# Gated cross-attention and a mixture of experts: the attention part rewritten for two heads in the two row halves of PE

## The chip, the cores and the metric

The kernel runs on one core of a Trainium2 chip. What counts is the device time of one launch in microseconds. PE is the matrix engine (TensorE), DVE the vector engine, ACT the scalar engine, POOL is GpSimd, and SP is the queue that issues the DMAs here.

## What is computed

```python
# x (4, 1024, 256); ctx (4, 154, 256); 16 heads of 16
q = layernorm(x) @ Wq.T / 4;  k = ctx @ Wk.T;  v = ctx @ Wv.T       # per head
d = clip(i - j, -4, 4) + 4                                           # i query, j key
scores = q @ k.T + (q @ p_params)[i, d];  scores = where(i >= j, scores, -1e30)
x = x + tanh(g_xattn) * (softmax(scores) @ v) @ Wo.T
h = layernorm(x);  s = sigmoid(h @ gate_w.T)      # 8 experts, 4 chosen through groups, plus a shared one
y = sum over chosen e of w_e * (silu(h @ Wg[e]) * (h @ Wu[e])) @ Wd[e] + shared(h)
x = x + tanh(g_ffn) * y
```

With 154 keys and 1024 queries, only the first 158 queries see a mask or a bias that depends on the distance; from then on every distance is clipped, and the bias of distance 4 is folded into the keys (`rel[:, 2 * DIST:]` is added to them). Two tiles of 128 queries per batch item, tiles 0 and 1, need corrections.

## The kernel before

A batch item has 1024 queries in two halves of 512. Attention runs in 8 units, one per batch item `b` and half `h` (`u = 2b + h`); an even unit (h = 0) holds the two corrected tiles. A unit has 20 steps on PE, five for each group of four heads: four score products with the keys as stationary operand and 512 queries moving (256 in an even unit), and one short chunk for the keys beyond 128, of four heads together (`score`, L892). ACT takes the exponential of each (L503), and PE multiplies by the values in four strips of 32 columns (`values`, L938 and L942). In the same steps PE works ahead: from step 3 on, two products a step give the scores of the next unit the other way round (queries stationary), only for the row maxima (`max_scores`, `stack_scores`, L877), through a ring of three PSUM banks that DVE empties (`maximum`, L604). Transposes of x (L811), queries (L853), keys (L822) and values (L837, L839) of the unit after next, the transposes of the maxima (L889, step 19) and the output projection of the unit before (L953, step 19) are put between the steps by hand. Each engine follows a list of steps of its own; PE, ACT and DVE run in order, so that one late wait holds up all that stands behind it.

Matmul operands are split in a high and a low part of type fp32r, and three products replace one in fp32. Heads go in stacks of two: `qs` holds for a stack 96 rows (two heads of 16 dimensions, in three copies: high, low, high), `km` the keys of both heads in 308 columns, block-diagonal, so that one product over 96 rows gives both heads; rows 96 to 127 carry the negated maxima, picked by one-hot rows in `ks`. The copies are made by DMAs from `qh`, `ql` (`q_stack`, 12 DMAs of 128 KB a unit) and from `km` (`k_stack`).

In an even unit the two corrected tiles go another way: ACT copies their scores from PSUM to `sx` (L486), POOL builds the band of bias corrections `d0`, `d1` from the products with `p_params` that stand in eight further columns (`near`, L388 to L411), DVE adds them and takes the maxima (`tile0`, `tile1`, L619 to L640), POOL and DVE subtract these, and PE transposes the result back into the score banks (L917, L922). The units of items 1 and 2 run in a loop (`Fori`), the others are written out.

The softmax divisors travel through DRAM and come back inverted and broadcast (`divisors`, 8 DMAs to `at`); DVE multiplies (`divide`, L671), PE projects, and DVE adds to x (L678). Behind attention, PE first projects unit 6, then turns to the experts' transposes (L1418), router (L1426) and 72 expert items of 24 matmuls each.

## Time and profile before

| | us |
|---|---|
| median of 3 runs | 726.85 (726.72 to 727.78) |
| profiled execution | 730.77 |
| its span | 728.7 |
| PE busy | 619.2 (85%) |
| DVE busy | 458.8 (63%) |
| ACT busy | 276.1 (38%) |
| POOL busy | 178.3 (24%) |

The busy times and all rows are of the one profiled execution. A busy PE is modelled: a matmul's record holds its latency too, so durations of neighbours overlap, and the rate is read from start to start. PEld are the loads of the stationary operand. In the name of a matmul, 96\*128 are the rows and columns of the array that it uses, and 96x308 what moves through. An fp32 matmul leaves two records.

### The profile page before, as it was taken

Reading aid. Unit: us, or ns where it says so; the run is one execution under the profiler, and the core shown is the slowest. Engines: PE = TensorE matmul, PEld = TensorE weight load, DVE = VectorE, ACT = ScalarE, POOL = GpSimd, SP = SyncE. Lnnn points to the kernel's source line nnn. Section 1 sums busy time; section 2 is a strip of 40 time slices with the busy share of each in tenths; the row PEclk is TensorE's granted clock in tenths of the full one; section 3 lists DMA queues with packets and bytes.
Section 4 is the critical chain, followed back from the end, with each engine's and each line's share of the span. In section 5 each row is a group of like instructions: output and inputs, shape, how many; then the busy total and the mean of one; then the engine's idle time right before and its main releaser. Section 6 shows DMA issues by size and latency. Waiting matters only on the chain.

```text
span 728.7 us, 10636 instructions
## 1 busy us (share of the span) xinstructions
PE 619.2 (85%) x3384; PEld 485.6 (67%) x3384; DVE 458.8 (63%) x884; ACT 276.1 (38%) x501; POOL 178.3 (24%) x177
## 2 busy tenths in 40 slices
PE   2665968788978987878667999999999999999997
PEld 2544745566645755554345888888888887888886
DVE  3677657868587758761277575756657475765653
ACT  2432456334733455344351422333242332324222
POOL 2151005300341007100111232232324223232222
PEclk9976989999989999999869999999999999999999
DMA  6850233524252333473212022031212202121220
GB/s 223 210 133 23 45 73 88 124 46 98 60 130 62 74 86 88 106 231 74 47 31 86 32 66 81 2 102 43 87 58 73 72 8 94 43 87 59 74 73 29
DMA packets 39856, 58.65 MB, mean 80 GB/s; under 512 B 7984, under 2 KB 21040, under 8 KB 39792
## 3 DMA queue, kind: packets, MB, share of 16 engines
q1 hardware_dynamic: 39824, 58.25, 28.9%
q8 instruction: 17, 0.28, 0.2%
q14 instruction: 15, 0.12, 0.0%
HBM read 31.76 MB, written 4.85 MB: 50 GB/s over the span
## 4 chain that ended last, share of the span: by engine, by line
issue 49%; PE 21%; DVE 11%; POOL 8%; DMA 5%; ACT 3%; SPq 2%; DVEq 0%; POOLq 0%; ACTq 0%
POOL hl L1172 4%; PE oT L938 3%; PE smax L877 3%; PE sT L918 3%; PE oT L942 3%; DMA qs<-mt 3%; DVE mx L604 2%; PE work L822 2%; SPq L296 2%; POOL d L399 2%; DVE mx L632 1%; PE sT L917 1%; DMA at<-rden_d 1%; PE work L853 1%; PE work L811 1%
## 5 line engine op out<-in xcount | busy, mean ns | idle before, releaser
L1172 POOL TENSOR_TENSOR hl<-sg,hh 128x512 fp32r<-128x512 f32 x72 | 93.2, 1296 | 249.6 <-ACT hh L1215 249.6
L503 ACT ACTIVATE ex<-sT 128x512 f32<-128x512 f32 (+1 forms) x160 | 91.9, 593 | 156.2 <-PE sT L918 130.7
L1209 ACT ACTIVATE sg<-pg 128x512 f32<-128x512 f32 x72 | 43.1, 598 | 199.2 <-PE pu L1455 198.4
L877 PE MATMUL smax<-km,qs 96*128 96x308 f32 (+1 forms) x244 | 86.9, 393 | 26.3 <-DVE mx L604 19.0
L604 DVE TENSOR_REDUCE mx<-smax 128x2 f32<-128x308 f32 x185 | 81.0, 472 | 35.8 <-PE smax L877 34.8
L877 PEld LDWEIGHTS smax<-km,qs 96*128 96x128 f32 x244 | 48.7, 209 | 60.5 <-DVE mx L604 35.4
L1470 PE MATMUL py<-wxl,hh 128*128 128x256 f32 x288 | 81.9, 284 | 4.2 <-DVE x L1353 3.1
L1470 PE MATMUL py<-wxh,hl 128*128 128x256 f32 x288 | 80.8, 281 | 0.0
L1470 PE MATMUL py<-wxh,hh 128*128 128x256 f32 x288 | 80.6, 280 | 0.0
L1341 DVE TENSOR_TENSOR sg<-cwb,sg 128x512 f32<-128x512 f32 x64 | 66.6, 1040 | 10.8 <-DMA cwb<-cwt_d 7.9
L1336 DVE TENSOR_TENSOR sg<-pu,sg 128x512 f32<-128x512 f32 x72 | 49.2, 684 | 28.4 <-ACT sg L1209 26.9
L918 PE MATMUL sT<-qs,ks 128*128 128x256 f32 (+1 forms) x128 | 53.4, 434 | 13.0 <-DMA qs<-mt 11.7
L1455 PE MATMUL pg<-x2l,wxh 128*128 128x512 f32 x144 | 60.3, 419 | 4.1 <-issue 4.1
L1470 PEld LDWEIGHTS py<-wxl,hh 128*128 128x128 f32 x288 | 54.3, 188 | 10.2 <-DVE x L1353 5.4
L1455 PE MATMUL pu<-x2l,wxh 128*128 128x512 f32 x144 | 57.9, 402 | 0.0
L1455 PE MATMUL pu<-x2h,wxl 128*128 128x512 f32 x144 | 57.8, 401 | 0.0
L1455 PE MATMUL pg<-x2h,wxh 128*128 128x512 f32 x144 | 57.6, 400 | 0.0
L1455 PE MATMUL pg<-x2h,wxl 128*128 128x512 f32 x144 | 57.5, 399 | 0.0
L1455 PE MATMUL pu<-x2h,wxh 128*128 128x512 f32 x144 | 57.3, 398 | 0.0
L1470 PEld LDWEIGHTS py<-wxh,hl 128*128 128x128 f32 x288 | 54.2, 188 | 2.7
L1470 PEld LDWEIGHTS py<-wxh,hh 128*128 128x128 f32 x288 | 54.6, 190 | 0.0
L1215 ACT CAST hh<-sg 128x512 fp32r<-128x512 f32 x72 | 44.0, 611 | 9.6 <-DVE sg L1341 9.3
(154 smaller groups left out, 1125.8 us busy)
## 6 DMA issues: line engine op xcount, KB each, us to landing
cwb<-cwt_d SPq DMA_DIRECT2D x64, 256.0 KB, 3.3
qs<-qh SPq DMA_DIRECT2D x64, 128.0 KB, 2.5
qs<-ql SPq DMA_DIRECT2D x32, 128.0 KB, 2.5
at<-rden_d SPq DMA_DIRECT2D x64, 64.0 KB, 2.2
out<-x SPq DMA_DIRECT2D x8, 512.0 KB, 4.3
ks<-km SPq DMA_DIRECT2D x16, 231.0 KB, 3.4
wx<-in_wx SPq DMA_DIRECT2D x9, 384.0 KB, 6.2
x<-in_x SPq DMA_DIRECT2D x3, 1024.0 KB, 8.6
```

Of the source, the lines that this page charges most:

```text
L503: nc.scalar.activation(ex[:, g % 2, i % 5, q0:HALF], ST[i % 2][:, q0:HALF], ACT.Exp).then_inc(exp_s, 1)
L604: nc.vector.reduce_max(mx[:, m_tile(h, p), 2 * stk:2 * stk + 2], banks[q % len(banks)][:, 0:PAIR].rearrange("p (j k) -> p j k", j=2), AX_X)\
L877: last_one = nc.tensor.matmul(bank[:, 0:width], qs[0:96, s, tile * P:(tile + 1) * P], km[:, s, 0:width], start=True, stop=True)
L918: last_one = nc.tensor.matmul(out[:, q0:HALF], ks[:, s, j * KL:j * KL + P], qs[:, s, q], start=True, stop=True)
L938: nc.tensor.matmul(OT[32 * j:32 * j + 32, :], va[:, 4 * g + j, :], ex[:, g % 2, j, :], start=True, stop=True)
L1172: nc.gpsimd.tensor_tensor(hl[:, i % R, :], sg[:, i % R, :], hh[:, i % R, :], ALU.subtract).then_inc(hl_done, 1)
L1209: nc.scalar.activation(sg[:, i % R, :], PG[i % RG][:], ACT.Silu).then_inc(sg_s, 1)
L1215: nc.scalar.copy(hh[:, i % R, :], sg[:, i % R, :]).then_inc(hh_s, 1)
L1336: done = nc.vector.tensor_tensor(sg[:, i % R, :], PU[i % RG][:], sg[:, i % R, :], ALU.mult)
L1341: nc.vector.tensor_tensor(sg[:, i % R, :], cwb[:, e % RC, :], sg[:, i % R, :], ALU.mult)\
L1455: last = nc.tensor.matmul(out_[:], wa[:, e, w], xa[:, u, c, :], start=first, stop=(c == C - 1 and wa is wxh and xa is xh))
L1470: last = nc.tensor.matmul(y, ha[:, i % R, q], wa[:, e, 2 * C * I:XW], start=(e == 0 and s == 0 and j % 2 == 0), stop=(e == NE1 - 1 and s = ...
```

## The change

The attention part is rewritten; the experts keep their items. In the diff:

- The heads of a stack lie apart: one in rows 0 to 63, the other in rows 64 to 127 of `qs` and `ks` (48 rows of high, low, high, two rows with the maxima's high and low part, zeros up to 64). A stack's scores are two products over 50 rows each, in the two halves (`score_pair`), of 124 keys and always 512 queries; the short chunk takes the other 30 keys. The products for the maxima (`fill`) are four in a step for steps 0 to 15, of 154 columns over 48 rows, into two banks that one reduction of DVE empties; the next `fill` waits for that reduction. Score banks are three instead of two, exponentials are kept in nine places.
- Corrections: POOL makes the bands `d0`, `d1` in a high and a low part, causal mask included, from products of their own (`relative`, 12 of 32 columns); PE adds them to the scores with the identity as the other operand (`added`, and the second part of `fill`). `sx`, the copies by ACT and the additions and subtractions on it are gone.
- Queries and keys are written to DRAM and read back in the new order (`q_store`, `q_stack`, `k_stack`), into three buffers for queries and two for keys. Keys are projected in 4 products instead of 16.
- In the head, the loads of x for items 1 to 3 come behind the stacks and six DMAs that write zeros to the unused rows (14 rows of 16 KB each); DVE waits for all three before its first reduction.
- The loop is gone: all units are written out. The maxima's transposes are in step 17, the output projections in 18 and 19. The divisors come back in one DMA, and POOL divides.
- Behind attention, the experts' first transposes are ahead of the projection of unit 6, and what DVE does for the router comes behind its first statistics.

```diff
-        sp.wait_ge(kv_in, 3 * 16)
-        for i in range(1, B):
-            sp.dma_start(x1[:, i * NT:(i + 1) * NT, :], t["x"][i]).then_inc(x_in[i], 16)
...
+        def q_store(u, part):
+            sp.dma_start(q_d[u, part], (qh, ql)[part][:].rearrange("p c n -> p (c n)").bitcast(F32)).then_inc(qd_out, 16)
+        def q_stack(u):
+            sp.wait_ge(qd_out, 32 * (u + 1))
+            if u > 2:
+                sp.wait_ge(st_ps, NEV * (u - 2))
+            for r in range(3):
+                rows = q_d[u, r % 2].rearrange("(s d) (a n) -> a d s n", d=HD, a=2)
+                for a in range(2):
+                    at_row = ROW * a + HD * r
+                    sp.dma_start(qs(u)[at_row:at_row + HD, :, :].bitcast(F32), rows[a]).then_inc(qs_in, 16)
...
+        def m_stack(u):
+            sp.wait_ge(mT_s, u + 1)
+            for a in range(2):
+                for part in range(2):
+                    at_row = ROW * a + KQ + part
+                    sp.dma_start(qs(u)[at_row:at_row + 1, :, :].bitcast(F32),
+                                 mt[H * part + a:H * (part + 1):2, :].bitcast(F32)).then_inc(ms_in, 16)
...
+        sp.wait_ge(q_hi, 2)
+        q_store(0, 0)
+        sp.wait_ge(work_free, freed("q", 0, 1))
+        q_store(0, 1)
+        q_stack(0)
+        sp.wait_ge(pool_set, 6)
+        k_stack(0)
+        zeros = k2[0:ROW - KS, :, :].rearrange("p s k -> p (s k)").bitcast(F32)
+        for i in range(RQ):
+            for a in range(2):
+                sp.dma_start(q_buf[i][ROW * a + KS:ROW * (a + 1), :, :].rearrange("p s n -> p (s n)").bitcast(F32)
+                             .rearrange("p (r k) -> p r k", r=4),
+                             zeros.unsqueeze(1).broadcast_to([ROW - KS, 4, NSTK * P])).then_inc(fill_in, 16)
+        for i in range(1, B):
+            sp.dma_start(x1[:, i * NT:(i + 1) * NT, :], t["x"][i]).then_inc(x_in[i], 16)
+        sp.wait_ge(v_ps, 1)
+        sp.dma_start(ctxb[:], t["ctx"][1]).then_inc(c_in, 16)
+        sp.wait_ge(work_free, freed("q", 1, 1))
+        q_store(1, 0)
+        q_store(1, 1)
+        q_stack(1)
+        m_stack(0)
...
+            nc.vector.reduce_max(mx[:, tile, 4 * sp:4 * sp + 4].rearrange("p (s a) -> p a s", a=2),
+                                 SM[:, :, 0:PAIR].rearrange("p a (s k) -> p a s k", s=2)[:, :, :, 0:keys],
+                                 AX_X).then_inc(mx_s, 1)
...
         for i in range(1, B):
             dve.wait_ge(x_in[i], 16)
+        tile_stats(2)
+        norm_stats(2)
+        for f in range(NFILL):
+            maximum(0, f)
+        minus_max(0)
+        max_out(0)
         dve.wait_ge(g_set, 1)
...
+        def fill(u, f):
+            h, b = u % 2, u // 2
+            tile, sp = fill_of(h, f)
+            if f == 0:
+                pe.wait_ge(qs_in, 6 * 16 * (u + 1))
+                pe.wait_ge(ks_in, 6 * 16 * (b + 1))
+            if u > 0 or f > 0:
+                pe.wait_ge(mx_s, NFILL * u + f)
+            edge = tile if h == 0 else 2
+            keys = P if edge == 0 else KL
+            for s in (2 * sp, 2 * sp + 1):
+                for a in range(2):
+                    rows = slice(ROW * a, ROW * a + KQ)
+                    last_one = nc.tensor.matmul(SM[:, a, s % 2 * KL:s % 2 * KL + keys], qs(u)[rows, s, tile * P:(tile + 1) * P],
+                                                ks(b)[rows, s, 0:keys], start=True, stop=True)
+            if edge < 2:
+                if f % 4 == 0:
+                    pe.wait_ge(d_s, NDS * b + (NDS if edge == 0 else 3))
+                for a in range(2):
+                    both = SM[:, a, 0:PAIR].rearrange("p (s k) -> p s k", s=2)
+                    heads = slice(4 * sp + a, 4 * sp + 4, 2)
+                    for part in range(2):
+                        if edge == 0:
+                            last_one = nc.tensor.matmul(both[:, :, 0:P], idr[:], d0[part][:, heads, :], start=False, stop=True,
+                                                        skip_group_check=True)
+                        else:
+                            last_one = nc.tensor.matmul(both[:, :, KM:KL], idr[:], d1[part][:, heads, 0:K1], start=False,
+                                                        stop=True, skip_group_check=True)
             last_one.then_inc(sm_ps, 1)
...
+        def added(out, keys, q, corrections):
+            for part in corrections:
+                last = nc.tensor.matmul(out[0:keys, q], part, idr[:, q.start % P:(q.stop - 1) % P + 1], start=False,
+                                        stop=True, skip_group_check=True)
+            return last
...
+        def score_pair(u, s):
+            n = NI * u + 5 * (s // 2) + 2 * (s % 2)
+            h, b = u % 2, u // 2
+            if n > 1:
+                pe.wait_ge(exp_s, n - 1)
+            if s == 0:
+                pe.wait_ge(ms_in, 64 * (u + 1))
+                pe.wait_ge(fill_in, 2 * RQ * 16)
+            for a in range(2):
+                rows = slice(ROW * a, ROW * a + KS)
+                last_one = nc.tensor.matmul(ST[0:KM, (n + a) % 3, :], ks(b)[rows, s, 0:KM], qs(u)[rows, s, :],
+                                            start=True, stop=True)
...
+                for a in range(2):
+                    last_one = added(ST[:, (n + a) % 3, :], KM, slice(0, P), [part[:, 2 * s + a, 0:KM] for part in d0])
+            last_one.then_inc(st_ps, 1)
...
+            out = ST[:, n % 3, :]
+            q0 = KM if h == 0 else 0
+            for k in range(2):
+                last_one = nc.tensor.matmul(out[:, q0:HALF], k2[:, 2 * g + k, :], qs(u)[:, 2 * g + k, q0:HALF],
+                                            start=(k == 0), stop=(k == 1))
+            if h == 0:
+                heads = slice(4 * g, 4 * g + 4)
+                added(out, P, slice(KM, P), [part[:, heads, :] for part in d0s])
+                last_one = added(out, P, slice(P, 2 * P), [part[:, heads, :] for part in d1])
+            last_one.then_inc(st_ps, 1)
...
+        def unit(u):
+            b = u // 2
+            ahead = u < NU - 2
             for i in range(NI):
-                seeks = 0 <= i - M0 < NM and (h == 0 or ahead)
-                score(b, h, i, start)
-                if seeks:
-                    max_scores(b + h, 1 - h, i - M0, 0)
-                if i in (1, 3) and carry:
-                    values(b - 1 + h, 1 - h, NG - 1, i // 2)
+                if i % 5 in (0, 2):
+                    score_pair(u, 2 * (i // 5) + i % 5 // 2)
+                elif i % 5 == 4:
+                    score_short(u, i // 5)
+                if i in (1, 3) and u > 0:
+                    values(u - 1, NG - 1, i // 2)
                 if i > 5 and i % 5 in (1, 3):
-                    values(b, h, i // 5 - 1, i % 5 // 2, start)
-                if seeks:
-                    max_scores(b + h, 1 - h, i - M0, 1)
-                if i in (5, 6) and ahead:
-                    transposes(u + 2, b, X_USE[h], (i - 5,))
-                if i in (7, 8) and ahead and h == 0:
-                    values_in(b + 1, b, V_USE, ((0, 1), (2, 3, 4))[i - 7])
-                if i in (9, 10, 11, 12) and ahead:
-                    queries(b, X_USE[h], Q_USE[h], (i - 9,))
-                if ahead and h == 0:
-                    keys(b + 1, b, K_USE, [s for s in range(NSTK) if K_STEP[s] == i])
-                if i == 19:
-                    if h == 0 or ahead:
-                        max_T(b + h, 1 - h, b, M_USE[h])
-                    if carry and (h == 0 or ahead):
-                        for pr in range(2):
-                            project(b - 1 + h, 1 - h, pr, b, Y_USE[h] + pr)
+                    values(u, i // 5 - 1, i % 5 // 2)
+                if u < NU - 1 and i < NFILL:
+                    fill(u + 1, i)
+                if ahead and i == K_PE and u % 2 == 0:
+                    keys(b + 1)
+                if ahead and i in X_PE:
+                    transposes(u + 2, X_PE.index(i))
+                if ahead and i in Q_PE:
+                    queries(u + 2, Q_PE.index(i) // 2, (Q_PE.index(i) % 2,))
+                if ahead and i == RV_PE:
+                    if u % 2:
+                        values_in(b + 1)
+                    else:
+                        relative(b + 1)
+                if i == NFILL + 1 and u < NU - 1:
+                    max_T(u + 1)
+                if i in (18, 19) and 0 < u < NU - 1:
+                    project(u - 1, i - 18)
```

## Rows read from the trace of the kernel before

**Rows 1.** Busy time by stage: length, then each engine's busy time, granted clock, DMA.

```profile
core 0: us, PE busy (x) PEld busy (x) DVE busy (x) ACT busy (x) POOL busy (x), PEclk, DMA share, GB/s
62.60:332.90 270.30, 220.94 (x1225) 154.48 (x1225) 192.05 (x363) 126.63 (x245) 52.62 (x60) 0.93 0.37 92
...
351.00:382.30 31.30, 19.54 (x59) 13.89 (x60) 18.16 (x52) 12.21 (x19) 3.91 (x5) 0.67 0.13 28
382.30:728.70 346.40, 332.94 (x1904) 287.12 (x1902) 211.91 (x394) 107.41 (x179) 102.27 (x84) 0.99 0.19 61
```

**Rows 2.** Waits of PE, 62.6 to 332.9: in total, times, longest.

```profile
PE smax L877 <- DVE mx L604: 19.0, 8, 3.9
...
PE sT L918 <- DMA qs<-mt: 11.7, 4, 5.4
```

**Rows 3.** Instructions in order of time, PE, 182 to 190: start, duration, instruction.

```profile
182.17 1.06 PE L938 MATMUL oT<-ex,va 128*32 128x512 f32 x8
183.17 0.73 PE L918 MATMUL sT<-qs,ks 128*128 128x512 f32 x2
183.74 0.31 PE L877 MATMUL smax<-km,qs 96*128 96x316 f32 x1
183.88 0.29 PE L880 MATMUL smax<-cmask,idr 128*128 128x256 f32 x1
184.01 0.81 PE L942 MATMUL oT<-ex,vb 128*128 128x384 f32 x2
...
189.84 0.60 PE L811 MATMUL work<-idr,xn 128*128 128x128 f32 x4
```

**Rows 4.** In order of time, 193.9 to 198, around a change to column strips.

```profile
193.93 3.65 POOL L399 TENSOR_TENSOR d<-relr,cst 128x2048 f32<-128x2048 f32 x1
...
195.72 0.39 PE L918 MATMUL sT<-qs,ks 128*128 128x512 f32 x1
...
195.95 0.30 PE L877 MATMUL smax<-km,qs 96*128 96x316 f32 x1
...
196.18 0.16 PEld L938 LDWEIGHTS oT<-ex,va 128*32 128x32 f32 x8 [0.27 <-issue]
196.18 1.06 PE L938 MATMUL oT<-ex,va 128*32 128x512 f32 x8
...
197.18 0.42 PE L877 MATMUL smax<-km,qs 96*128 96x316 f32 x1
...
197.44 0.39 PE L853 MATMUL work<-xth,wql 128*128 128x512 f32 x1
```

**Rows 5.** In order of time, the head up to the first score.

```profile
20.12 3.44 PE L822 MATMUL work<-ctxb,wk 128*96 128x154 f32 x24
...
21.65 1.38 SPq L267 DMA_DIRECT2D qs<-qh  x2
...
39.91 0.85 DVE L604 TENSOR_REDUCE mx<-smax 128x2 f32<-128x308 f32 x2
...
62.93 0.56 PE L918 MATMUL sT<-qs,ks 128*128 128x256 f32 x1
```

**Rows 6.** DMA issues of the page: KB each, median time to landing.

```profile
qs<-qh SPq DMA_DIRECT2D x64, 128.0 KB, 2.5
```

**Rows 7.** DMAs that load x, 0 to 30: duration of issue, first and last start.

```profile
L260 SPq DMA_DIRECT2D x<-in_x x3: 378/583/1469, 13.6 to 14.6; - x3
...
DMA to landing us min/median/max: 4.6/7.8/12.1
```

**Rows 8.** In order of time, between attention and experts.

```profile
355.45 1.40 DVE L1253 BATCH_NORM_STATS2 stats<-x 128x6 f32<-128x256 f32 x4
...
358.61 6.72 PE L953 MATMUL work<-wo,at 128*128 128x256 f32 x16 [4.37 <-DVE at L671]
...
372.38 0.80 PE L1426 MATMUL pm<-x2l,gst 128*128 128x512 f32 x1 [1.40 <-DVE x2l L1269]
```

More of the change, by code:

```diff
@@ L21 @@
 KL = 154
-K1 = KL - P
 KPAD = 160
@@ L431, in gpsimd @@
-        batches(pool, unit)
+        rotated(0)
+        near(0)
+        values(0)
+        rstd_of(2)
+        for u in range(NU):
+            unit(u)
+        return lambda: divide(NU - 2), lambda: divide(NU - 1)
     def scalar(act):
@@ L523, in scalar @@
[L523 to L537 removed]
+            nc.scalar.copy(kept(u)[:, g, :], OT[:]).then_inc(raw_s, 1)
```

1148 lines of the change are left out of this document (517 added, 631 removed).

## Prediction

> **What bounds the kernel now.** I read the busy time by stage first [rows 1]. It tells three things. The expert stage from 382.3 us on takes 346.4 us with PE busy 332.9 of them at a granted clock of 0.99; the change touches none of its loop, so it moves as a block. The middle of attention, from the first score to the last unit (62.6 to 332.9, 270.3 us for seven of eight units, about 39 us each), has PE busy 220.9, DVE 192.1, ACT 126.6: PE is the fullest engine and no other is near it, but PE also stands still for 49 us. What is left is a head of 62.6 us before the first score and a passage of 31.3 us between attention and the experts, in which PE is busy 19.5 us at a clock of 0.67. I then asked what PE waits for in the middle [rows 2]: 19.0 us for DVE to reduce the maxima, 11.7 us at the starts of units for the DMA that brings the negated maxima. Last I looked at single matmuls for prices [rows 3, 4], and at the head and the passage in order of time [rows 5 to 8]. So attention is bound by the order of work on PE, with two waits in it; the head is bound by a chain over ACT, DVE and POOL; and whatever the change does, 346 us stay.
>
> **Prices, at full clock.** Start to start: 512 columns in fp32r 0.23 us (195.72 to 195.95); 308 or 316 columns 0.14 (183.74 to 183.88); 256 columns 0.13 (183.88 to 184.01) [rows 3, 4]. An fp32 transpose of 128 columns 0.11 (four in 0.60 less the tail of the last) [rows 3]. Four heads' values in the four column strips of PE 1.0 (182.17 to 183.17). An fp32 key projection of 154 columns 0.29, as two records of 0.14 each (24 in 3.44) [rows 5]. No fp32r matmul under 256 columns stands in the trace, and none in the upper or lower half of the rows. Bounds for one of 154 or 128 columns: below, in proportion to the 308-column row, 0.07; above, the fp32 key row, 0.29. I take 0.12: a 256-column matmul with a new stationary block of 128 columns takes 0.13, so the block can be exchanged in that time, and the 308-column row is of the same operands. For a pair of heads in the two halves I take one such time, not two, since in the column strips the eight records of four heads run together (eight weight loads in 0.16 us [rows 4]).
>
> **What a change of tiling costs.** From full rows to strips: 195.95 to 196.18 is 0.23 for a matmul of 0.14, so 0.09 more. Back: 197.18 to 197.44 is 0.26 for one of 0.14, so 0.12 more for the next weight load, which could not be brought forward [rows 4]. Some 0.1 per change, then, between bounds of 0 (if halves need no such drain; the trace has column strips only) and 0.2. The Trainium skill says the same and against this change: its page TensorEngine Tiling (Array Packing), section Tiling Modes, has it that a change of tiling mode, not only of tile, drains the engine. By that rule every passage from halves to full rows is paid; the strips' rows agree, and halves no row shows.
>
> **Units, part by part.** Common to both versions, per unit: values, query projections, transposes of x, output projection. What differs, in us of PE:
> Even unit before: 16 heads of two transposes and a 256-column score, 16 x 0.34 = 5.4; four short chunks 1.4; 32 stacks of maxima 4.6; keys, 32 records of 0.14, 4.6: 16.0. After: 8 pairs of 512 columns 1.9; 32 corrections of 128 columns 3.8; four short chunks with four corrections 3.4; 32 pairs for the maxima 3.8; keys 4 x 0.29 = 1.2; the new relative products, 12 x 0.12 = 1.4: 15.5.
> Odd unit before: scores 3.7, short chunks 1.9, maxima with eight masks 5.6: 11.2. After: pairs 1.9, short chunks 1.9, maxima 3.8, 32 corrections to their edge tiles 3.8: 11.4.
> So the halving of scores is spent on corrections: 0.2 us saved per unit. The changes of tiling: fills alternate with values, chunks, corrections and projections in each of 16 steps, about 45 passages per unit against 8; 37 x 0.11 = 4.1 more. The waits: one reduction of 616 elements per step, in place of two of 308 (0.85 for two [rows 5]), on one pair of banks where there was a ring of three; a fill waits for the reduction of the step before, most of which lies under 1 us and more of other PE work: from 2.7 us per unit (19.0 over seven) to about 1. The maxima leave two steps earlier, before both output projections: of 1.7 us per unit (11.7 over seven) 0.5 stay. Late next is the query projection at step 4: its operand is subtracted on DVE only behind the reduction of the same step, 0.85 + 0.7 us: 1.0 more. Together -0.2 + 4.1 - 1.7 - 1.2 + 1.0 = +2.0 per unit, by 6.5 units (the first has no output projection, the seventh no projections ahead) +13. DVE loses the additions and subtractions on whole score tiles and the division, POOL and ACT their parts of it; none of that ends last, so beyond the waits it is worth nothing. Divisions go to POOL behind the band work (two of the 3.65 us row [rows 4], a mask of the same shape as much, and the small ones): about 15 of 39 us, done before the projection at step 18. Loops written out add instructions to fetch; no row prices it, 0 to 3 us, I take 0.
>
> **The head.** Before, three loads of x (1 MB each) are issued at 13.6 to 14.6 and the slowest lands after 12.1 us [rows 7]; the first score is at 62.93 [rows 5]. After, SP issues them only behind the stores of queries and keys to DRAM, the wait for these, six plus six stack loads and six zero fills of 224 KB. From the queries' end at 21.65 [rows 5]: store and return 2.5, the landing time of a stack load of 128 KB [rows 6], six loads at 0.6 each (two in 1.38 [rows 5]) to 28, keys' store and return to 31.5, six loads to 35, fills to 39, x to 41. Then 1.3 + 3 MB at the pace of the 12.1 us row: landed near 53. DVE waits for all three before its first reduction, then does 1.8 us of statistics: 54 or 55. PE stands with one fill made and its clock falls, as in the passage (0.67 [rows 1]). Sixteen fills then take turns with sixteen reductions, nothing overlapping: 0.85 reduction, 0.5 matmuls at half clock, 0.25 handing over, 1.6 x 16 = 26, and 1.0 for the corrections of eight: 33. At 87 come transposes, copy and DMA, about 4 (an estimate; PE's wait for such a DMA was 2.9 in the mean, 11.7 over four [rows 2]): first score at 91, 28 later. Low bound: x landed at 47, turns of 1.2: +12; high +36. I take +26.
>
> **The end.** DVE's statistics for the experts start at 355.45, having waited for ACT's last copy; PE does 16 records of output projection (6.72 us at half clock, 358.61 to 365.3) ahead of the transposes; the router starts at 372.38 [rows 8]. After, statistics wait for nothing (351), transposes come first, the division is on POOL after rstd near 357, projection until 364, router right behind: 8 us earlier, and the last unit, with three banks in place of two, perhaps 1. The weights' DMA stands ahead of the divisors in SP's queue and lands some 9 us into the last unit, early enough. I take -8 (-2 to -12).
>
> **Sum.** 730.8 (span 728.7 and 2.1 around it) + 26 + 13 - 8 = 761.8. The profiled execution was 3.9 above the median shown, 726.85, so 758.
>
> **Rivals.** (a) PE runs free. If a change between halves and full rows costs nothing (-4.1), a pair of fills passes in 0.08 (-1.3), no fill waits (-1.0) and the clock stays up (0.93 in the middle: -1.5), a unit is 5.9 us shorter, -38 in all; with a head of +22 and -8: 730.8 - 24 - 3.9, about 703, faster. For it: 49 us of PE's idleness and DVE's load of 192 us are what the change removes. Against: the head. (b) Short fp32r matmuls at the fp32 price: 32 pairs at 0.26 and 128-column corrections at 0.21, +6.4 per unit, +42: 800. For it: no row under 256 columns; against: nothing in the 308-column row hints at it. (c) The halves don't run side by side, so the change doesn't do what it says: 32 x 0.12 and 8 x 0.23 more, +5.7 per unit, +37: 795. The Trainium skill is against (c): TensorE: Matmul & The Clock Gate, Part 3, measures four row tiles of 32 at 3.07 times one. (d) Head and units cancel, 727: the head at +12 with units at -0.6 each.
>
> **How the numbers follow.** Forecast 758, chance 0.40, own range 738 to 778. (a) 0.29, (b) 0.17, (c) 0.09, (d) 0.05. 0.2% of this kernel is 1.5 us, about what its measurement tells from no change. Faster: (a) and the low edge of (d), 0.31; same 0.04; slower 0.65. Range 700 to 802: below lies part of (a), above part of (b).
>
> **What would show it.** Head: first reduction right after x's third landing near 53, fills and reductions in turn, first score near 91; if it is under 75 the forecast falls. Units: start to start of a fill behind a full-row matmul 0.1 over the same without a passage; two heads' records starting within 0.02 (else (c)); 154 columns at 0.12 and not 0.26 (else (b)); unit length 41 and not 34 (else (a)). End: transposes ahead of the projection, router near 13 us after the last score instead of 21.

## The result, and the profile after

| | before | after |
|---|---|---|
| median of the runs, us | 727.3 (4 runs, 726.7 to 729.0) | 895.8 (4 runs, 893.8 to 899.1) |
| profiled span, us | 728.7 | 892.4 |
| head, to the first exponential | 63.5 | 115.3 |
| units 0 to 6 | 269.9 (38.6 each) | 386.8 (55.3 each) |
| last unit | 18.1 | 16.3 |
| from there to the experts' first gate | 30.8 | 27.8 |
| experts | 346.4 | 346.2 |

The ratio is 1.2322 (95% interval 1.2284 to 1.2361): 168 us slower, where 31 were forecast. Rows are of one execution of each kernel; those of e7 below are of its slowest (798.9 us, its median is 788.3), so that a comparison with them overstates what another kernel gained on it by up to 10 us. The span grew by 163.7: head +51.8, units +116.9, the end -4.8. The stages of after, with the columns of [rows 1]:

```profile
114.00:502.10 388.10, 315.95 (x1544) 195.41 (x1546) 163.46 (x254) 105.41 (x207) 79.28 (x67) 0.71 0.35 64
518.40:546.20 27.80, 16.66 (x59) 12.39 (x60) 16.80 (x43) 11.78 (x18) 8.64 (x8) 0.75 0.23 52
546.20:892.40 346.20, 333.81 (x1904) 288.05 (x1902) 212.36 (x398) 107.31 (x179) 102.06 (x84) 0.99 0.19 61
```

DVE did become lighter (163 us against 192 in [rows 1]), and the time did not follow. The granted clock in the units fell from 0.93 to 0.71, that is, PE spent more than half of the time at 1.2 GHz and the rest at 2.4. What PE waited for in the units of after, as [rows 2]:

```profile
PE sT L883 <- issue: 35.7, 6, 9.1
PE work L775 <- DVE xn L590: 19.3, 3, 10.3
PE work L809 <- DVE xtl L595: 9.7, 6, 1.8
PE smax L841 <- DVE mx L642: 5.9, 16, 0.5
PE sT L883 <- DMA qs<-mt: 5.1, 1, 5.1
```

The wait for reductions fell from 19.0 to 5.9 us, as forecast. The first row is the first score of a unit, which waits for the maxima's DMA; "issue" only means that the profile found no releaser. In order of time, PE and SP's queue show it:

```profile
268.78 2.69 SPq L271 DMA_DIRECT2D qs<-q_d  x6
...
271.66 1.89 PE L937 MATMUL work<-wo,at 128*128 128x256 f32 x8
...
271.91 2.72 SPq L294 DMA_DIRECT2D qs<-mt  x4
...
274.13 1.94 PE L937 MATMUL work<-wo,at 128*128 128x256 f32 x8
...
285.17 0.79 PE L883 MATMUL sT<-qs,ks 50*124 50x512 f32 x2 [9.10 <-issue]
```

Six copies of a query stack (1.5 MB) are issued just ahead of the four small DMAs; the last of the six lands 12.9 us after its own issue, 15.1 after that of the first. The second row of waits is this, DVE, POOL and PE in order of time:

```profile
170.21 0.80 DVE L642 TENSOR_REDUCE mx<-smax 128x4 f32<-128x616 f32 x1 [5.07 <-PE smax L841]
170.50 3.63 POOL L425 TENSOR_TENSOR d0h<-relr_h,cst 128x2048 fp32r<-128x2048 f32 x1
170.92 11.89 DVE L590 TENSOR_SCALAR xn<-x,mv,rstd 128x256 f32<-128x256 f32 x4
...
174.21 4.49 POOL L432 TENSOR_TENSOR d0h<-d0h,cst 128x2048 fp32r<-128x2048 f32 x1
178.66 3.69 POOL L425 TENSOR_TENSOR d0l<-relr_l,cst 128x2048 fp32r<-128x2048 f32 x1
...
182.97 1.08 PE L775 MATMUL work<-idr,xn 128*128 128x128 f32 x4 [10.32 <-DVE xn L590]
```

Four operations of 0.41 us took 11.89 together: the first three each end 0.15 us after one of POOL's, the fourth takes 0.40 again. The head in order of time, where [rows 5] had the reductions at 39.91:

```profile
44.08 11.31 SPq L352 DMA_DIRECT2D qs<-k  x6
...
55.44 7.34 SPq L356 DMA_DIRECT2D x<-in_x  x3
...
72.05 1.41 DVE L575 BATCH_NORM_STATS2 stats<-x 128x6 f32<-128x256 f32 x4 [39.96 <-DMA x<-in_x]
...
76.21 0.71 PE L841 MATMUL smax<-ks,qs 48*128 48x154 f32 x4 [0.89 <-DVE mx L642]
76.96 0.80 DVE L642 TENSOR_REDUCE mx<-smax 128x4 f32<-128x616 f32 x1 [0.81 <-PE smax L841]
77.81 0.71 PE L841 MATMUL smax<-ks,qs 48*128 48x154 f32 x4 [0.90 <-DVE mx L642]
```

The turns are 1.6 us, as forecast. What came late is x. Last, PE at the full clock around its changes of tiling, and the end (compare [rows 8]):

```profile
261.85 0.45 PE L841 MATMUL smax<-ks,qs 48*128 48x154 f32 x4
...
262.14 0.43 PE L883 MATMUL sT<-qs,ks 50*124 50x512 f32 x2
...
262.50 0.32 PE L868 MATMUL sT<-idr,d0h 128*124 128x128 f32 x1
...
262.65 0.27 PE L868 MATMUL sT<-idr,d0l 128*124 128x128 f32 x1
...
262.87 0.27 PE L868 MATMUL sT<-idr,d0l 128*124 128x128 f32 x1
...
263.20 0.45 PE L841 MATMUL smax<-ks,qs 48*128 48x154 f32 x4
...
517.94 1.40 DVE L1234 BATCH_NORM_STATS2 stats<-x 128x6 f32<-128x256 f32 x4 [3.00 <-PE sT L900]
...
529.15 5.02 PE L937 MATMUL work<-wo,at 128*128 128x256 f32 x16
...
533.83 0.59 PE L1406 MATMUL pm<-x2l,gst 128*128 128x512 f32 x1
```

Two heads' scores pass in 0.36 us (262.14 to 262.50), a passage included, where two of 512 columns one behind the other would take 0.46; four matmuls of 154 columns in 0.29. So halves run side by side; a pair of 154 columns costs 0.15 and a correction of 128 columns 0.11, not 0.26 and 0.21.

**A unit taken apart.** For units 1 to 6 I added up the time from each PE record's start to the next one's, by the clock at its start. What is over 0.8 us counts as a stop (less 0.3 for the record; values at 1.2 GHz count as stops in part). "PE at 2.4 GHz" prices each kind of record by its mean at the full clock. Us per unit:

| | PE at 2.4 GHz | added by 1.2 GHz | stops | sum |
|---|---|---|---|---|
| before | 29.6 | 1.0 | 8.0 | 38.6 |
| after | 34.3 | 6.2 | 14.9 | 55.4 |

The stops are firm, the split of the rest hangs on the pricing: with means by the kind of the next record too, or with all that ran at 2.4 GHz taken as it stands, PE's part of after comes out at 32 to 37 us and the clock's at 3 to 8, those of before at 29 to 30 and about 1. PE's own work is 4.7 longer by the table, 3 to 7 by the other pricings (forecast 3.9: 4.1 for passages less 0.2). The stops were forecast 1.9 shorter and are 6.9 longer; the clock, for which the units had no term, takes 5.2. So of the 15 us a unit by which the forecast fell short, the stops are 9 and the clock is 5.

### The profile page after: what moved, and what is told of

It reads as the page before. It is cut to its first block, busy times and chain, and to the rows that moved or that the text cites. A ratio compares the mean times of both kernels' runs of the same rounds, so it can differ in the third digit from the quotient of the medians.

```text
span 892.4 us, 10515 instructions
## 1 busy us (share of the span) xinstructions
PE 715.7 (80%) x3744; PEld 528.2 (59%) x3744; DVE 428.1 (48%) x774; ACT 245.0 (27%) x442; POOL 216.5 (24%) x190
## 4 chain that ended last, share of the span: by engine, by line
issue 40%; PE 38%; DVE 10%; POOL 5%; DMA 4%; SPq 3%; ACT 1%; POOLq 0%; ACTq 0%; DVEq 0%
PE smax L841 7%; PE oT L919 5%; DVE mx L642 4%; PE work L809 4%; PE oT L924 4%; PE sT L868 4%; POOL hl L1148 3%; PE sT L883 3%; PE work L937 3%; DVE xn L590 3%; PE sT L900 2%; PE work L775 1%; PE smax L851 1%; DMA k_d<-kl 1%; PE smax L854 1%
## 5 line engine op out<-in xcount | busy, mean ns | idle before, releaser
L642 DVE TENSOR_REDUCE mx<-smax 128x4 f32<-128x616 f32 (+1 forms) x128 | 100.4, 784 | 214.6 <-PE smax L841 168.2
L527 ACT ACTIVATE ex<-sT 124x512 f32<-124x512 f32 (+2 forms) x160 | 88.0, 586 | 330.9 <-PE sT L868 202.7
L841 PEld LDWEIGHTS smax<-ks,qs 48*128 48x128 f32 x512 | 54.8, 257 | 126.2 <-DVE mx L642 75.4
L841 PE MATMUL smax<-ks,qs 48*128 48x154 f32 (+1 forms) x512 | 74.8, 381 | 61.6 <-DVE mx L642 45.0
L883 PE MATMUL sT<-qs,ks 50*124 50x512 f32 x128 | 39.0, 604 | 40.8 <-issue 35.7
L1317 DVE TENSOR_TENSOR sg<-pu,sg 128x512 f32<-128x512 f32 x72 | 49.2, 683 | 28.5 <-ACT sg L1188 27.2
L919 PE MATMUL oT<-ex,va 124*32 124x512 f32 x256 | 50.8, 878 | 4.0 <-ACT raw L514 3.1
```

What stands on the lines that cost most here:

```text
L527: nc.scalar.activation(ex[0:rows, n % NEX, q0:HALF], ST[0:rows, n % 3, q0:HALF], ACT.Exp).then_inc(exp_s, 1)
L642: nc.vector.reduce_max(mx[:, tile, 4 * sp:4 * sp + 4].rearrange("p (s a) -> p a s", a=2), SM[:, :, 0:PAIR].rearrange("p a (s k) -> p a s k ...
L841: last_one = nc.tensor.matmul(SM[:, a, s % 2 * KL:s % 2 * KL + keys], qs(u)[rows, s, tile * P:(tile + 1) * P], ks(b)[rows, s, 0:keys], sta ...
L883: last_one = nc.tensor.matmul(ST[0:KM, (n + a) % 3, :], ks(b)[rows, s, 0:KM], qs(u)[rows, s, :], start=True, stop=True)
L919: last_one = nc.tensor.matmul(OT[32 * j:32 * j + 32, :], va[0:KM, 4 * g + j, :], ex[0:KM, (n + j) % NEX, :], start=True, stop=True)
L1317: done = nc.vector.tensor_tensor(sg[:, i % R, :], PU[i % RG][:], sg[:, i % R, :], ALU.mult)
```

## Experiments

Times are medians of a kernel's runs; ratios, with their 95% intervals, are against before, run beside them. The edits are given in short. e5, e6, e7, e9, e10, e13 and e14 leave work out or read other data, so what they compute is not the reference's; the others compute everything.

**Head and order (e1 to e4).** e1 moves the loads of x behind that of wo; e2 moves the maxima's DMAs to ScalarE's queue; e3 normalises a unit earlier; e4 does all three.

```diff
+ e1: for i in range(1, B): sp.dma_start(x1[...], t["x"][i])      # behind wo's load
+ e2: if i == 18 and u < NU - 1: m_stack(u + 1)                    # on ScalarE, not SP
+ e3: if i == 19 and u < NU - 3: normalised(u + 3)                 # DVE; was step 0, u + 2
```

> The three 1 MB loads of x are issued right behind the weights again, ahead of the stacks; nothing else is changed. Theory A (the head is set by DVE's wait for x behind the slow stack and zero-fill DMAs): first reduction at 47 instead of 73.8 (when the key stack has landed), first exponential near 89 instead of 115, total 896 - 26 = 870. Rival B (the stacks themselves are the limit, x in front only pushes them back by its 9 to 10 us): first reduction at 56 to 60, total 880 to 886. Rival C (the head is off the path): 896.

> The four DMAs of the negated maxima go through ACT's queue, behind the exponential of step 18, instead of SP's queue behind the six query-stack loads. Theory A (they wait in SP's queue behind 13 us of stack loads): PE's stops at the starts of units (2.8, 6.7, 9.5, 8.3, 4.7, 5.9 us) fall to under 2 each, -27 us, and with PE's clock up more often another -5 to -10: 858 to 868. Rival B (a 16 KB DMA into a single partition is slow by itself): the stops stay, 896. Rival C (both queues share the 16 DMA engines, so the stack's packets still go first): half of it, 880.

> The normalisation of x moves from step 0 of unit u to step 19 of unit u-1, so that in odd units it no longer meets POOL's large band operations. Theory A (DVE's two-operand-rate operation on SBUF is held up by POOL's running instruction, four of them took 11.9, 4.0 and 8.2 us instead of 1.4): all four take 1.4 us, PE's stops before the transposes (10.7, 2.8, 7.0) go, -18 us, 876 to 880. Rival B (another DVE operation meets the bands instead, or PE then waits for the maxima): under -6 us, 890.

> All three edits at once. If the three causes are separate their gains add: 26 + 27 + 18 = 71, and with fewer stops PE's clock, 0.72 in the units, comes up: 800 to 825. If a common limit stands behind them (PE's own work at 154 columns, changes between halves and full rows) units stay above 48 us and the total above 840.

Measured: e1 874.4 (ratio 1.198, 1.192 to 1.203), its first exponential at 89.4 where after has 115.3: x is half of the head's loss. e2 892.5 (1.223, 1.213 to 1.232): no gain clear of noise; the stops at the units' starts are still 2.4 to 7.1 us (26.2 in all, 35.7 in after) and end 1 to 2 us after the stack's last copy has landed (from unit 2 on), so it was not SP's order alone: the small DMAs land behind the stack's from another queue too. e3 877.3 (1.202, 1.194 to 1.209): theory A's time, but not its mechanism, since in two units four normalisings still took 13 us. e4 869.5 (1.189, 1.182 to 1.195): 26 us where 71 were expected. The collision had only moved, as in e3: behind the residuals of step 19 the normalising met POOL again.

```profile
250.30 13.05 DVE L590 TENSOR_SCALAR xn<-x,mv,rstd 128x256 f32<-128x256 f32 x4
```

**Causes taken away (e5 to e7).**

```diff
+ e5: if u > 2: return                          # in q_stack: no stacks from unit 3 on
+ e6: if b > 0: return                          # in POOL's near: edge tensors of batch 0 stay
+ e7: e1, e5 and e6 together
```

> Leaves out the copies of queries from DRAM into the stacks from unit 3 on (six of 256 KB a unit, 48 of them in the kernel, 18 left); scores are then made from old queries. Nothing else is taken out. Theory A (the stack's 13 us of transfers, 6 x 2.2 us, stand ahead of the maxima's DMAs and make PE stop 4.7 to 9.5 us at the start of a unit): those stops go to under 1 us, the units from 55.3 to about 49, and the kernel from 896 to 856 (five or six units x 6 to 7). Theory B (the 16 KB DMAs into one partition are slow by themselves, 2.8 us each, or the maximum itself comes late): the stops stay above 4 us, the kernel within 10 us of 896. With A the granted clock in the units, 0.72 on average, rises too if it is the stops that lower it (over 0.80); it stays near 0.72 if it is the kind of work.

> Leaves out POOL's building of the edge tensors for batches 1 to 3 (near(b), six wide operations of 3.6 to 4.6 us in units 1, 3 and 5); the edge tensors stay those of batch 0, and PE's corrections read them as before. Theory A (DVE's normalising is held while POOL runs a wide operation: 11.9 us for four tensor_scalar at 170.9 where 1.38 is usual, and PE stands for it): the three normalisings in those units take under 2 us, PE's waits for xn there (10.7, 2.8, 7.0 us) go, and the kernel falls by 15 to 25 us, to some 875. Theory B (the normalising is late for another reason, rstd or x): DVE's four operations still take over 4 us in one of the units, and the kernel stays within 8 us of 896.

> The loads of x issued behind that of wo, the query stacks from unit 3 on and POOL's edge tensors of batches 1 to 3 left out, all three in one kernel; output is not the reference's. In the traces so far a unit of after is 55.2 us: about 34 that PE's instructions take at the full clock, 6 that the half clock adds to them, 15 of stops (before: 30 + 1 + 8). Theory A (the stops come from these causes, and the stops lower the clock): stops fall to about 7 and the clock comes back to over 0.85, units of 42 to 44, and the kernel near 896 - 26 - 6 x 11 = 800. Theory B (the clock falls because of the short instructions and the half-row matmuls themselves): stops fall as in A, but the clock stays under 0.78, units near 48 and the kernel near 830. Theory C (a common limit, as three changes together gave 26 us of 71): 850 or more.

Measured: e5 853.3 (1.162, 1.147 to 1.176); PE's wait in the first row above falls from 35.7 to 7.9 us, the granted clock in units 1 to 6 rises from 0.73 to 0.80; in turn PE's wait for the normalising grows from 19.3 to 29.9, which hides part of the gain until e7 takes both away. e6 869.1 (1.190, 1.183 to 1.198). The twenty-four normalising operations in after and in e6 (duration min/median/max in ns):

```profile
L590 DVE TENSOR_SCALAR xn<-x,mv,rstd x24: 399/407/4651, 116.7 to 406.1; 128x256 f32<-128x256 f32 x24
```

```profile
L590 DVE TENSOR_SCALAR xn<-x,mv,rstd x24: 404/407/410, 116.9 to 382.4; 128x256 f32<-128x256 f32 x24
```

Nothing but POOL's edge tensors was taken out (six tensor_tensors a batch item, of which three take 3.6 to 4.5 us, not six as expected, and two small copies), and the 4.65 us are gone: theory A of e6 is shown. The Trainium skill, page SBUF — State Buffer, section SBUF: two separate sides, has that GpSimd and certain VectorE operations take one pair of ports for a whole instruction and block the other meanwhile; the trace agrees. e7 788.3 (1.080, 1.071 to 1.088), 108 us less than after, more than e1, e5 and e6 apart (21 + 43 + 27): what e4 missed was not a common limit but a collision and the stacks. The time is theory A's; the clock in the units, 0.82, lies between A (over 0.85) and B (under 0.78). A unit, by the columns of the table above: 34.3 + 3.6 + 5.8 = 43.7 us.

**What is left at PE (e9, e10).**

```diff
- rows = slice(ROW * a, ROW * a + KS)
+ rows = slice(0, P)          # e9, on e7: scores, and fills from unit 3 on
- if h == 0:
+ if False:                   # e10, on e7: no edge corrections in score_pair
```

> As e7_no_both, but the matmuls of the score pairs, and from unit 3 on those of the fills, run over all 128 rows of PE instead of a half (both heads' products are added up; the rows of ones under the keys are zero and the queries a quarter of their size, so that the exponential stays finite). The number of matmuls is the same; two of a pair no longer run side by side, and PE never changes its tiling for rows. Side by side saves, by e7's trace at the full clock, 8 pairs x 0.21 us of scores and some 32 pairs x 0.06 to 0.11 of fills, 3.5 to 5 us a unit. Theory A (each passage between halves and whole array costs 0.12 to 0.2 us, 37 of them a unit): 4.5 to 6 us come back, so a unit is within 1.5 us of e7's 46.6 and the kernel within 10 us of 788. Theory B (passages cost little, the extra PE time is the added instructions): the kernel is 20 to 35 us slower. Theory C (matmuls in half the rows also hold the clock down): the mean granted clock in the units, 0.83 in e7, goes above 0.92 and the kernel is 10 us or more faster.

> As e7_no_both, without the two matmuls of 128 columns per head that add the edge tensors to the score pairs of even units (32 a unit in units 0, 2, 4, 6; those of short scores and fills stay). Theory A (they cost what the trace shows start to start at the full clock, 0.11 us each, and one passage of tiling each pair): 3.5 us for the matmuls; the passage is only moved to the fill or the values behind, so 3.5 to 4.5 us come off each even unit and 16 us off the kernel, to about 772. Theory B (they are hidden, since a ring or the exponential sets the pace): within 4 us of 788. Theory C (with them the clock goes up too, or a passage more is saved): 25 us or more.

Measured: e9 774.3 (1.061, 1.056 to 1.066), 14 us faster than e7 though PE has more to do: theory C. The units of e7 and of e9:

```profile
145.70:407.60 261.90, 243.42 (x1330) 148.71 (x1332) 123.21 (x215) 90.75 (x179) 28.36 (x36) 0.82 0.20 51
```

```profile
136.20:382.50 246.30, 224.75 (x1332) 156.37 (x1336) 125.82 (x215) 90.89 (x179) 28.45 (x36) 0.94 0.20 54
```

With as many matmuls and the same queues around them the clock (the column before the last two) goes from 0.82 to 0.94 when they fill all rows; over the whole kernel it was 0.861 to 0.873 in the three runs of e7 and 0.911 to 0.918 in those of e9. A unit is 37.2 + 1.2 + 2.6 = 41.0: side by side saves 2.9 us of PE (0.4 to 4.1 by the other pricings) and the clock takes it back. The stops column falls by 3.2 mostly because records at 1.2 GHz count in it; the idle time that the trace gives PE is 2.9 us a unit in e7 and 3.4 in e9.

What a passage costs is read from single records at 2.4 GHz, in e7 and then in e9:

```profile
386.22 0.43 PE L886 MATMUL sT<-qs,ks 50*124 50x512 f32 x2
386.58 0.32 PE L871 MATMUL sT<-idr,d0h 128*124 128x128 f32 x1
386.75 0.27 PE L871 MATMUL sT<-idr,d0l 128*124 128x128 f32 x1
...
386.96 0.27 PE L871 MATMUL sT<-idr,d0l 128*124 128x128 f32 x1
387.28 0.45 PE L844 MATMUL smax<-ks,qs 48*128 48x154 f32 x4
```

```profile
371.11 0.67 PE L886 MATMUL sT<-qs,ks 128*124 128x512 f32 x2
371.61 0.22 PE L871 MATMUL sT<-idr,d0h 128*124 128x128 f32 x1
371.67 0.27 PE L871 MATMUL sT<-idr,d0l 128*124 128x128 f32 x1
...
371.89 0.27 PE L871 MATMUL sT<-idr,d0l 128*124 128x128 f32 x1
372.16 0.67 PE L844 MATMUL smax<-ks,qs 128*128 128x154 f32 x4
```

From the scores to the fourth correction it is 0.74 us in e7 and 0.78 in e9, and e7 has the way back to the halves (0.09 and more) still to go: the passages eat what two heads side by side save. In e7 the scores' last 512 columns, with the passage to all rows, take 0.36 (0.23 in e9, medians of 11 and 14), the first correction 0.16 instead of 0.06; a fill's last 154 columns ahead of all rows take 0.20 instead of 0.11, and 512 columns over all rows ahead of the halves 0.33 instead of 0.23. So a passage costs 0.09 to 0.13, and the first matmul over all rows behind it 0.06 to 0.10 more: the forecast's 0.11 holds, and 37 passages are 3.3 to 4.8 us a unit, near theory A. The rows' zeros and smaller queries of e9 are another difference; no run tells them apart from the rows in use. e10 771.2 (1.056, 1.049 to 1.064): 17 us less than e7, theory A's 16; PE at 2.4 GHz falls by 2.6 us a unit.

**The stack's 13 us (e8, e13, e14, e16).**

```diff
+ e8:  q_rows(act, u + 2, (1,))                 # upper half from ScalarE, step 13
+ e13: src = qs(u + 1)[at_row:at_row + HD]      # from SBUF, not DRAM
+ e14: sp.dma_start(qs(u)[ROW*a:ROW*a + 2*HD], both[a])   # 32 rows per copy
+ e16: sp.dma_start(qs(u)[ROW*a:ROW*a + KQ], rows[a])     # 48 rows, third store
```

> Computes everything. From unit 2's stacks on, the three copies into the upper row half go out from the ScalarE queue behind exponential 13, the three into the lower half stay on SyncE's, so two queues work on a stack. Theory A (a copy's 2.2 us is a limit of the one queue): the stack lands in about 7 us instead of 13, the stops at the start of the units fall to under 3 us and the kernel by 20 to 30 us. Theory B (the limit is the 16 DMA engines' packets, 266 ns for 2 KB into 16 partitions at a time, and two halves at once may even spread better): the packets take 400 ns or more each, the stack lands in 12 to 14 us as before and the kernel stays within 10 us of 896. Theory C (16 partitions are the limit, not the engine): packets of two halves at once stay at 266 ns each and overlap, so it is as A.

> From unit 3 on each of the six copies of a query stack reads the same rows of the neighbouring stack in SBUF instead of DRAM (scores are then made from old queries); destinations, sizes, packets of 2 KB and their order are those of after. Theory A (reading DRAM makes a packet slow): packets go from 266 to about 150 ns, as in the kernel before, whose stacks came from SBUF, and a stack lands in 8 us instead of 13. Theory B (16 partitions written at a time are the limit): packets stay at 250 ns or more and the stack at 13 us. The kernel's time follows: some 20 us less with A, within 10 us of 896 with B.

> From unit 3 on the four copies of 16 rows that bring high and low parts are two copies into 32 rows of 512 KB each, from DRAM, in packets of the same 2 KB (the rows are not the right ones, since their order in DRAM is another); the two copies of the third part stay at 16 rows. Theory A (DRAM): packets stay near 260 ns in all six parts, the stack at 13 us. Theory B (the number of partitions a copy writes into): the packets of the two wide copies take 130 to 160 ns, the two narrow ones 260, so the stack lands in 4 x 1.2 + 2 x 2.2 = about 9 us, and the kernel is 10 to 20 us faster than 896.

> Computes everything. As e12_shift, but the query stacks go another way: queries are stored in DRAM with high, low and high part as 48 neighbouring rows (three stores of 512 KB instead of two), and a stack is two copies into 48 rows of 768 KB each, both on SyncE's queue; ScalarE issues none. Theory A (the packet's time goes with the partitions a copy writes into: 266 ns at 16, about 155 at 32): some 110 to 150 ns a packet, the stack lands in 5.5 to 7.5 us instead of 13; the third store costs under 2 us; ScalarE's stop of 5 us in odd units is gone and the stops for the maxima's DMAs are under 3 us. Units of 44 to 46, the kernel at 780 to 792. Theory B (the longer store delays the stack as much as the wide copies save): within 5 us of e12's 802. Theory C (PE, at the half clock in a third of the units, sets the pace): the stops go and the time stays above 795.

Measured: e8 871.8 (1.194, 1.184 to 1.203): 24 us less, the time of A, but with stacks near B's: from the first issue to the last landing a stack takes 11.9 to 13.5 us, in after 14.5 to 15.6 (132 GB/s with both halves under way, measured in e12). It also leaves 6.2 to 10.5 us ahead of the maxima's DMAs, where that was 3.1 to 6.9 in after (from unit 2 on). Which of the two helps, no run tells; it is not that three copies stand ahead in SP's queue instead of six, since SP's three land only 0.4 to 1.0 us before ScalarE's. e13 895.0 (1.229, 1.218 to 1.240): no change, a stack in 14.8 to 15.4 us, so DRAM is not the cause. Its packets were of 16 KB, not of 2 KB as expected, so the packets' size isn't either. e14 887.6 (1.219, 1.212 to 1.225): 8 us less where 10 to 20 were expected, and a stack in 12.8 to 13.4 us, not 9, though its wide copies are as fast as theory B has them. Busy time by stretch again; the last column is GB/s, in stretches in which next to nothing but stack copies runs; in order: before (copies into 32 rows, SBUF to SBUF), after (16 rows), e14 in its 32-row and in its 16-row copies:

```profile
258.00:263.00 5.00, 3.05 (x16) 1.09 (x14) 4.64 (x12) 1.08 (x2) 0.10 (x1) 0.93 0.95 226
```

```profile
270.50:283.00 12.50, 5.50 (x28) 4.46 (x28) 2.18 (x3) 1.30 (x3) 11.96 (x12) 0.86 1.05 114
```

```profile
257.80:262.90 5.10, 5.10 (x23) 2.75 (x24) 2.86 (x10) 1.08 (x2) 4.58 (x8) 0.50 0.93 193
264.20:267.80 3.60, 3.60 (x11) 2.69 (x10) 0.41 (x1) 0.00 (x0) 0.00 (x0) 0.63 0.92 106
```

The engines are all busy in each (share 0.92 to 1.05); 16 rows take 106 to 114, 32 rows 193 to 226 GB/s. e16, with 48 rows, should have been faster still and was not: 143 GB/s, and with its third store the stack left only 0.8 to 3.7 us ahead of the maxima's DMAs, 860.2 (1.181, 1.176 to 1.187). All three of its theories missed. The Trainium skill, page SBUF — State Buffer, section Door 1: The DMA port swizzle, has 4 ways into SBUF under rows 0 to 15, 8 under 0 to 31, and rows 32 to 47 on the first 4 again, at 27.2 GB/s each: 109 for 16 rows and 218 for 32, with which 106 to 114, 193 and 226 agree within 12%; 129 GB/s in e13 and 132 in e12, also in copies of 16 rows, lie above the 109, and no run says why. For 48 rows 163 is an estimate from that page's figures (two thirds of the bytes on four ways), above the 143 measured.

**Versions that compute everything (e11, e12, e15, e17, e18).**

```diff
+ e11: e1 + e8; DVE: if i == NFILL + 1 and u < NU - 3: normalised(u + 3)   # step 17
+ e12: e11; Q_PE, Q_HI, Q_LO = (5, 6, 7, 8), (7, 9), (8, 10); RV_PE, RV_OUT = 11, 12
+ e15: e12, ScalarE's copies behind exponential 15
+ e17: e12, q_d as (NU, NSTK, 2 * HD, C * HALF), copies into 32 + 16 rows
+ e18: e17, ScalarE's copies behind exponential 15
```

> Computes everything. Three changes to after: the loads of x behind that of wo; DVE normalises for unit u + 2 at step 17 of unit u - 1 (behind the maxima's copy, where POOL has nothing wide to do) instead of at step 0 of unit u; and the upper halves of the query stacks go out from ScalarE's queue as in e8. Theory A (POOL's wide operations hold DVE, and e3 and e4 only moved the collision: at step 19 the normalising came behind the residuals and ran into them again, 13.05 us for four at 250.3 of e4): normalising takes under 2 us everywhere, the stops at xn and at DVE's maxima of 12 us are gone, and the kernel is near 896 - 26 (head) - 20 (stack) - 25 (normalising) = 825 to 835. Theory B (DVE is late for another reason): the waits come back at step 17 or in the reductions, and the kernel stays at 850 or more.

> As e11_early_two, with PE's query projection one step later (steps 5 to 8 instead of 4 to 7, what follows it one step later too), so that DVE's difference of x, 1.76 to 2.11 us of stop at step 4 of six units, is done when PE comes to it. Theory A (the stop is pure waiting at an instruction placed too early): 1.8 us less a unit and some 11 us less than e11, the clock a little higher with it. Theory B (the query stack leaves a step later in return, 2.5 us, and the stop comes back at the next unit's start at the maxima's DMAs): the same time as e11 within 4 us.

> As e12_shift, with ScalarE's three copies of the query stack issued behind exponential 15 instead of 13. In e12 ScalarE stood up to 5.8 us there for the store of the queries (issued at 213.19 after exponential 13 at 207.39) and PE stood 4.71 and 6.11 us for the output bank behind it. Theory A (those two stops are only that): about 8 to 12 us less than e12's 802, near 792. Theory B (the copies leave later, and the maxima's DMAs and the next fills wait for them in return): within 4 us of e12.

> Computes everything. As e12_shift, but high and low part of the queries stand in DRAM as 32 neighbouring rows per stack, so a half of a stack is one copy into 32 rows (512 KB) and one into 16 (256 KB), the upper half on ScalarE's queue, the lower on SyncE's; the stores stay two of 512 KB. Theory A (a copy into 32 rows starting at 0 or 64 reaches twice as many ways into SBUF as one into 16; the 48 rows of e16 load the ways of rows 0 to 15 a second time with rows 32 to 47): packets near 130 to 150 ns in the wide copies, the stack in 8 to 10 us instead of 11 to 13, the stops for the maxima's DMAs (2.6 to 4.5 us in e12) under 2 us, the kernel at 785 to 795. Theory B (it is not the copies' width but the queue they stand in or the number of rows at once): the stack takes 11 us or more and the kernel stays within 5 us of 802.

> As e17_rows32, with ScalarE's copies behind exponential 15 instead of 13, as e15 was to e12. e15 took away ScalarE's stops of 4.7 and 6.1 us, but its stacks landed later and the stops for the maxima's DMAs grew to 4.0 to 8.9 us: +17 us. Theory A (with a faster stack the later issue costs less than ScalarE's stops): within 5 us of e17 or faster. Theory B (whatever leaves later than step 13 stands ahead of the maxima's DMAs): 8 us or more slower than e17.

Measured: e11 826.3 (1.131, 1.123 to 1.139), theory A; no normalising takes over 0.42 us. e12 801.6 (1.096, 1.087 to 1.105): 25 us less where 11 were expected; the wait at the query projection is gone and the clock went from 0.835 to 0.859 in the whole kernel. What stops e12 in odd units is ScalarE, whose copies wait for the store of the queries (its rows in order of time; the exponential before them ended at 207.98):

```profile
213.19 1.32 ACTq L252 DMA_DIRECT2D qs<-q_d  x3
214.61 0.49 ACT L530 ACTIVATE ex<-sT 128x388 f32<-128x388 f32 x1 [6.63 <-issue]
```

e15 818.5 (1.124, 1.119 to 1.129): theory B's mechanism, but 17 us slower than e12 where B had no more than 4; that stop is gone and those for the maxima's DMAs are 3.6 to 8.5 us. e17 793.8 (1.089, 1.079 to 1.098): the stack in 9.8 to 11.0 us (e12: 12.3 to 13.0), no stop over 0.8 us at a unit's start from unit 2 on, but now PE waits for ScalarE in each unit, by the waits of PE from 90 to 500:

```profile
PE oT L929 <- ACT raw L517: 15.0, 6, 4.8
PE oT L929 <- ACT raw_first L517: 13.2, 4, 7.1
```

Its interval overlaps e12's. e18 818.7 (1.126, 1.118 to 1.134): B again. No version reached the kernel before.

## Why the prediction was wrong

The sign was right, the size far outside the range of 700 to 802. The mechanism of the units was missed: what was foreseen there (passages between halves and full rows, halves side by side, shorter waits for reductions) came about as priced, and three costs that the prediction put near nothing, or had no term for, are with the late x of the head most of the error. By its own steps:

- **Experts, end.** Experts 346 us: right. The end came 4.8 us earlier, forecast 8: statistics at once, transposes ahead of the projection, the router 17 us after the last score where 13 were forecast. PE stood 4.74 us for DVE's second difference of x ahead of the projection, which the step had left out.
- **Prices and passages.** Halves side by side: right, rivals (b) and (c) are out. A pair of 154 columns takes 0.15 where 0.12 was taken. The passages were put at 0.11 and the records of e7 beside e9 give 0.09 to 0.13: right. PE's own work came at about +4.7 where +3.9 was forecast.
- **The wait for maxima's DMAs: the step that failed.** I let it shrink from 1.7 to 0.5 us a unit because the maxima leave earlier, and did not ask what stands ahead of them. It is 5.1 (35.7 over seven). The six stack loads were priced at 0.6 us each from a copy of 128 KB into 32 rows [rows 5]; they have 256 KB and go into 16 rows: 2.2 each, 13 a stack. The 1.38 us in [rows 5] are moreover the time in which SP issues two copies, not in which they arrive; after issues its six in 2.69 us, and they have landed after 15.1. That 0.6 fits such a copy all the same (128 KB at 226 GB/s are 0.58) was luck. e5 shows the cost, 43 us; e14's rates show that the rows written to set the pace of a copy, though its stack came only 2 us sooner.
- **POOL "worth nothing": failed.** I priced POOL's time and found it had room. Its wide operations block DVE's normalising, for 4 to 12 us in each of units 1, 3 and 5; e6 shows 27 us. [rows 4] had such a POOL row of 3.65, and I did not look at what DVE did beside it.
- **The clock had no term in the units.** It takes 5.2 us a unit. Part follows the stops (e5: 0.73 to 0.80 with one cause removed), part the half rows (e9: 0.82 to 0.94).
- **The head.** +52, forecast +26. The turns, their number and the 33 us behind x were right (first reduction at 73.8, first exponential at 115.3, 41 us, with 5 us for the maxima's DMA and the unit's start); x was forecast at 53 and landed at 72, since the six stack loads took 15 us from first issue to last landing instead of 3.6 and the zero fills 11 instead of 4. In e1 the first exponential is 26 us earlier, and the kernel 21 us shorter.
- **The query projection** waited 1.4 us a unit where 1.0 was forecast: right, yet e12 shows it was worth 4 a unit, with the clock.

**Open.** How much of e9's clock is the rows in use and how much its data; what part of e8's gain is the quicker stack and what part its earlier start; why copies into 48 rows run at 143 GB/s; and whether 4 us a unit of stops in e17 can go without new ones (with the stops gone, 34.2 + 2.4 us a unit, e17's columns of the table above, would bring about 750: an estimate; not tried).

## What to carry to other kernels

Price a DMA by bytes and by how many rows it is written into, from a row with the same number of rows, by the time to landing and not by that of the issue, and ask of every small DMA what stands ahead of it on the engines, whatever its queue. An engine with idle time isn't free: look what its neighbour does while its long operations run. And when an edit packs more work side by side in part of the array, give the clock a term of its own, and set its passages against what side by side saves: here they ate it.

## What the runs showed of the hardware

- Copies into 16 SBUF rows ran at 106 to 114 GB/s in packets of 2 KB from DRAM (after, e14), at 132 when two queues issued them (e12) and at 129 in packets of 16 KB from SBUF (e13); into 32 rows at 193 (from DRAM, e14) and 226 (from SBUF, before); into 48 at 143 (e16).
- A VectorE tensor_scalar of 0.41 us over SBUF took up to 4.65 while GpSimd ran wide tensor_tensors; two reductions from PSUM beside them took their usual 0.80.
- With the same count of matmuls, all rows in use brought a granted clock of 0.94, half rows 0.82 (e9 and e7, whose operands differ too).
- A change between row halves and all rows cost PE 0.09 to 0.13 us at 2.4 GHz, and the first matmul over all rows 0.06 to 0.10 more (e7 beside e9).
